# The opening of a fused cross-attention kernel, written in another order

## What is computed

```python
x = x + tanh(g_xattn[0]) * xattn(layernorm(x), ctx, ctx, Wq, bq, Wk, bk, Wv, bv, Wo, bo)
x = x + tanh(g_ffn[0]) * ffn(layernorm(x), Wg, W1, b1, W2, b2)

# xattn
qh = (q @ Wq + bq) per head;  kh = (k @ Wk + bk) per head;  vh = (v @ Wv + bv) per head
attn = softmax(qh @ kh.T / sqrt(16), axis=-1)
return concat(attn @ vh) @ Wo + bo
```

## Time and profile before

| | us |
|---|---|
| median of 3 runs | 1028.3 |
| lowest to highest of them | 1026.89 to 1028.31 |
| profiled execution, its own time | 1025.19 |
| span of the profiled execution | 1023.4 |
| first T product (step -1 opens) | 104.30 |
| first and last output copy of the attention | 120.8, 585.3 |

### The profile page before, as it was taken

One profiled execution on the slowest core, in us unless ns is written; L12 is line 12 of the kernel. 1 busy time (PEld: TensorE's weight loads), 2 busy tenths in 40 slices (PEclk: granted clock), 3 DMA queues, 4 the chain that ended last, 5 costly groups with the idle time before them and its releaser, 6 DMA issues. The chain is left out here.

```text
span 1023.4 us, 23194 instructions
## 1 busy us (share of the span) xinstructions
PE 879.9 (86%) x8875; PEld 697.4 (68%) x8875; DVE 670.4 (66%) x1852; ACT 615.2 (60%) x1312; POOL 242.1 (24%) x208
## 2 busy tenths in 40 slices
PE   4766999999999999999998720169999999999995
PEld 2433676676776676677676510159999999999995
DVE  5424677777777877877878568846647566574440
ACT  1546777777777777777775520056847658476571
POOL 6940000000000000000000031243645556465313
PEclk9989999999999999999999955579999999999998
DMA  5236655655755645745642030132352533525203
GB/s 144 65 75 132 148 124 123 163 122 125 164 119 127 163 114 134 161 114 134 156 106 50 25 101 0 45 121 59 96 130 48 129 100 75 129 47 144 32 11 37
DMA packets 96211, 104.65 MB, mean 102 GB/s; under 512 B 11744, under 2 KB 92272, under 8 KB 96112
## 3 DMA queue, kind: packets, MB, share of 16 engines
q1 hardware_dynamic: 84128, 88.50, 34.6%
q0 software_dynamic: 10752, 14.69, 8.3%
q10 hardware_dynamic: 1232, 0.12, 0.1%
HBM read 39.60 MB, written 14.68 MB: 53 GB/s over the span
## 5 line engine op out<-in xcount | busy, mean ns | idle before, releaser
L361 DVE TENSOR_REDUCE a_nm<-a_pS 112x1 f32<-112x375 f32 x512 | 264.4, 543 | 103.9 <-PE a_pS L537 100.8
L250 ACT ACTIVATE a_P<-a_pT 128x448 f32<-128x448 f32 x384 | 209.1, 546 | 134.5 <-PE a_pT L531 133.6
L537 PE MATMUL a_pS<-a_kst,a_qst 96*112 96x375 bf16 x512 | 151.1, 333 | 3.6 <-DVE a_nm L361 3.0
L531 PE MATMUL a_pT<-a_qst,a_kst 98*128 98x112 bf16 x1536 | 139.0, 213 | 0.1
L531 PEld LDWEIGHTS a_pT<-a_qst,a_kst 98*128 98x128 bf16 x1536 | 107.0, 99 | 40.8 <-issue 8.2
L1250 PE MATMUL e_p<-w2h,e_hh 128*128 128x256 f32 x448 | 128.2, 286 | 0.0
L1250 PE MATMUL e_p<-w2h,e_hl 128*128 128x256 f32 x448 | 126.1, 282 | 0.0
L1250 PE MATMUL e_p<-w2l,e_hh 128*128 128x256 f32 x448 | 126.1, 281 | 0.0
L851 POOL MEMSET r_factors<- 128x1 f32 x15 | 0.6, 102 | 530.1 <-POOLq L62 530.1
L1105 POOL DMA_INDIRECT out_dram<-e_y,e_idx x56 | 88.4, 1578 | 137.5 <-ACT e_y L1134 130.7
L260 ACT ACTIVATE a_kp<-a_pK,a_bk 128x375 bf16<-128x375 f32 x192 | 109.4, 570 | 5.2 <-PE a_pK L564 3.8
(11 more groups left out here) (198 smaller groups left out, 1556.1 us busy)
## 6 DMA issues: line engine op xcount, KB each, us to landing
a_kst<-a_kp SPq DMA_DIRECT2D x192, 192.0 KB, 3.6
w<-in_L_ffn_W_dram SPq DMA_DIRECT2D x16, 1024.0 KB, 7.4
a_qst<-a_qp SPq DMA_DIRECT2D x96, 112.0 KB, 3.8
a_craw<-in_ctx_dram SPq DMA_DIRECT2D x32, 128.0 KB
a_xin<-in_x_dram SPq DMA_DIRECT2D x8, 448.0 KB, 3.9
a_xb<-in_x_dram SPq DMA_DIRECT2D x32, 112.0 KB, 3.0
out_dram<-a_x SPq DMA_DIRECT2D x32, 112.0 KB, 2.4
xn_scratch<-a_x SPq DMA_DIRECT2D x32, 112.0 KB, 2.6
```

Source lines behind the costliest of these rows:

```text
L250: act.activation(P[quad % 2][:, c, :], pT[u % 2][:, 0:4 * LQ], ACT.Exp).then_inc(exp_done, 1)
L361: dve.tensor_reduce(nm[:, h:h + 1], pS[h % 2][0:LQ, 0:LK], AXX, ALU.max, negate=True).then_inc(s_used, 1)
L531: last = pe.matmul(pT[u % 2][:, j * LQ:(j + 1) * LQ], kst[b % 4][:, h, c * 128:(c + 1) * 128], q_of(b, slice(None), h), start=True, stop=True)
L537: pe.matmul(pS[h % 2][0:LQ, 0:LK], q_of(b, slice(0, ROWS), h), kst[b % 4][0:ROWS, h, 0:LK], start=True, stop=True).then_inc(s_ready, 1)
```

## The change

Steps -12 to -2 of the loops are gone (`FIRST = -1`). In front of each engine's loop stands a loop over the query groups j = 0 to 7 of its own. After it, every engine has done for the main loop what it had done before: K of batches 0 to 3, the context transposes of 0 to 4, V of batch 0, all heads of batch 0 and heads 0 to 7 of batch 1 in the first score pass, and the transposed maxima of batch 0. In detail:

- Queries use one bank for each half, pO and pM0 (`pQ = [pO, pM[0]]`), and not two pairs. The third cut of each (`q_low`) is made by VectorE, from the bank.
- K of batches 0 to 3 is computed beside groups 1 to 4, its half t = 1 in bank pS0 and t = 0 in pK. Their semaphores `k_ready` and `k_cut` are one for each half. From batch 4 on all is in pK as before.
- The first score pass of batch 0 is beside groups 5 and 6, the first half of that of batch 1 beside group 7.
- VectorE normalises all of group 0 and the fourth batch of every other group; GpSimd does three batches of groups 1 to 7. GpSimd's fill of the ones rows of kst moves from groups 2 to 5 to groups 4 to 7.
- The xnT copies of groups 6 and 7 are ScalarE's.
- V of batch 0 is made beside group 5, both pieces in pM1. The context transposes of batches 0 to 3 are beside groups 0 to 3.
- SyncE loads two contexts early, and issues all six query stackings of a pair at once for pairs 0 and 1.

The diff, cut to its core:

```diff
-        pQ = [[pS[0], pS[1]], [pO, pM[0]]]
+        pQ = [pO, pM[0]]
...
-        FIRST, LAST = -12, B + 2
-        G, GROUP_0 = B // 4, -10
+        FIRST, LAST, G = -1, B + 2, B // 4
+        EARLY_K, DVE_COPIES = 4, 6
...
+        def k_bank(b, t):
+            return pS[0] if b < EARLY_K and t == 1 else pK
...
+            for j in range(G):
+                if live_q(j + 4):
+                    sp.wait_ge(xnt_ready, 2 * j + 2)
+                    x_group(j + 4)
+                if 2 <= j < 5:
+                    if j == 2:
+                        sp.wait_ge(pads_set, 2)
+                    stack_keys(j - 2)
+                if 1 <= j < 5:
+                    context(j + 1)
+                if j == 1:
+                    stack_queries(0, range(6))
+                if j == 4:
+                    stack_queries(1, range(6))
+            row_max(0)
...
+            for j in range(G):
+                kb = j - 1 if 1 <= j <= EARLY_K else None
+                if 2 <= j <= EARLY_K + 1:
+                    for t in range(2):
+                        k_part(j - 2, t, 2)
+                q_piece(j, 0, 0)
+                if j == 5:
+                    values(0, 0)
+                if kb is not None:
+                    k_part(kb, 0, 0)
+                if live_q(j + 2):
+                    root(j + 2)
+                q_piece(j, 0, 1)
+                q_piece(j, 1, 0)
+                if kb is not None:
+                    k_part(kb, 0, 1)
+                    k_part(kb, 1, 0)
+                if j == 5:
+                    values(0, 1)
+                if DVE_COPIES <= j + 1 < G:
+                    x_copies(act, j + 1)
+                q_piece(j, 1, 1)
+                if j < 4:
+                    ct_copy(j)
+                if kb is not None:
+                    k_part(kb, 1, 1)
...
+            x_statistics(0)
...
+            x_scale(0)
+            for b in range(4):
+                x_norm(0, b)
+            x_statistics(1)
+            x_copies(dve, 0)
+            x_scale(1)
+            for j in range(G):
...
+                if live_q(j + 2):
+                    x_statistics(j + 2)
+                if live_q(j + 1):
+                    x_norm(j + 1, 3)
...
+                maxima(0, 2)
+                if live_q(j + 2):
+                    x_scale(j + 2)
+                maxima(2, 5)
+                if j + 1 < DVE_COPIES:
+                    x_copies(dve, j + 1)
+                maxima(5, 6)
+                q_low(j, 0)
+                maxima(6, 8)
+                if j == 6:
+                    max_parts(0)
+                q_low(j, 1)
...
+                if j == 5:
+                    pe.wait_ge(kst_loaded[0], 96)
+                    pe.wait_ge(qst_loaded[0], 96)
+                    pe.wait_ge(k_cut[1], 3 * EARLY_K)
+                if j == 7:
+                    pe.wait_ge(kst_loaded[1], 96)
+                q_product(j, 0)
+                if kb is not None:
+                    keys(kb, 0, 0)
+                early_s(0, 2)
...
+                q_product(j, 1)
+                early_s(2, 3)
+                q_rest(j, 1, 0)
+                if kb is not None:
+                    keys(kb, 0, 1)
+                    keys(kb, 1, 0)
+                early_s(3, 5)
...
+                if live_q(j + 1):
+                    x_transposes(j + 1)
+                q_rest(j, 1, 1)
+                early_s(5, 6)
+                q_rest(j, 2, 0)
+                if kb is not None:
+                    keys(kb, 0, 2)
+                    keys(kb, 1, 1)
+                if j < 4:
+                    wait(pe, ct_copied, j)
+                    ct_transposes(j)
...
+                early_s(6, 8)
+                q_rest(j, 2, 1)
+                if kb is not None:
+                    keys(kb, 1, 2)
+            pe.wait_ge(ct_copied, 5)
+            m_transpose(0)
+            for t in range(2):
+                pe.wait_ge(q_cut[t], 3 * G)
```

More of the change, by code:

```diff
@@ L209, in _ @@
+                if live(m + 7):
+                    context(m + 7)
                 if live(m + 1):
@@ L552, in weighted, with keys @@
                     last.then_inc(o_ready, 1)
-            def keys(b, i):
-                t, part = divmod(i, 3)
-                wait(pe, k_cut, 6 * b + i)
+            def keys(b, t, part):
+                bank = k_bank(b, t)
+                if part > 0:
+                    pe.wait_ge(k_cut[t], 3 * b + part)
+                else:
+                    wait(pe, k_cut[0], 3 * b + (3 * t if b >= EARLY_K else 0))
+                    wait(pe, k_cut[1], 3 * b)
                 if part == 0:
@@ L609, in _ @@
                     if live(b):
-                        if u == 6 and b == 0:
-                            for t in range(2):
-                                pe.wait_ge(q_cut[t], 3 * (G - 1))
                         if u == 6:
```

303 lines of the change are left out of this document (155 added, 148 removed).

## The result

| | before | after |
|---|---|---|
| median (4 runs each, same chip), us | 1028.3 | 1001.75 |
| lowest to highest | 1026.89 to 1029.24 | 1000.14 to 1002.26 |
| profiled execution, its own time | 1025.19 | 1000.14 |
| span of it | 1023.4 | 998.4 |
| first T product | 104.30 | 76.44 |

The ratio is 0.9741, with a 95% interval of 0.9726 to 0.9755.

A forecast was written before the change was run, and what follows sets the result against it. TensorE bounds the main loop, waits behind ScalarE's K cuts the opening; 2.3 - 3.4 + (52.1 - 24.4) = 26.6 us saved, so 1028.3 - 26.6 = 1001.7, say 1002; range 998 to 1010.

The forecast's parts named there:

- What bounds it, and the sum: TensorE bounds the main loop, waits behind K cuts the opening; 2.3 - 3.4 + (52.1 - 24.4) = 26.6 us gained.
- The start: Start to group 1, VectorE normalising group 0: first query product at 12.3, group 1 at 20.9; gain 2.3 us.
- they will again: In the start: the two query products of group 0 take 5.82 us, as before.
- The K groups: Groups 1 to 4 with K: 6.8 us work plus 1.1 waiting, 7.9 each, 32.4 in all; range 6.8 to 9.5 each.
- Groups 5 to 7: Groups 5 to 7 with maxima, up to the first T product: 24.4 us, before 52.1; bounds 20.2 and 28.
- What is queued behind the new waits: SyncE's query and K stacking between x loads: costed at nothing; uncovered, each would delay its group up to 3 or 4 us.
- The first: Rival: TensorE's clock falls inside the new groups, three to six product pairs, 4.4 to 8.8 us: 1006 to 1011; chance 0.13.
- its step is TensorE's own time, so all of it should come through: Main loop: starts from the same finished pieces at an unchanged step, so the whole 26.6 us gain reaches the total.
- The second: Rival: ScalarE's order keeps K exposed in the groups, two of a batch's six waiting 1.77 us: +10, 1012; chance 0.06.
- The third: Rival: the low clock level holds through the opening, 20.9 to 77.7 us: +36, 1037, slower; chance 0.04.

## Why the prediction was right, step by step

**What bounds it, and the sum.** The main loop kept its pace, so what the opening gained came through, less 1.2 us in step -1, 0.5 over the 31 steps behind it, and 1.2 behind the attention. The first T product moved by 27.9 us where 26.6 was forecast, the span by 25.0. That the median agrees within 0.3 us is partly chance: the profiled execution came out at 1000.14, 1.5 above the forecast 998.6, and the median stands 1.6 above it in place of the assumed 3.1.

**The start.** Forecast: first product at 12.3, group 1 at 20.9, a gain of 2.3. Measured 11.83 and 19.67, a gain of 3.5. VectorE's block took 0.35 us (forecast 0.37), and with group 0 back on GpSimd 2.26 us were lost. Of the 1.2 us beyond, 0.5 lie ahead of the first product; 0.3 of them are there already when the inverse root of group 0 ends (7.80, before 8.14). The larger part, 0.9, comes from "they will again": the two products took 4.94 us (11.83 to 16.77), not 5.82, because the second ran mostly at the full rate. Over the other runs it took 1.81 to 3.11 us, so this is the luck of one execution, about 1 us wide.

**The K groups.** Forecast 7.9 apart and 32.4 in all, by a count of TensorE's issue (6.8) plus one exposed cut (1.1). Measured 7.85 for groups 2 and 3 and 32.0 in all, with 28.30 us busy and one wait of 0.8 a group, in groups 1 to 3 for the cut that was named. The outer two were off in opposite ways. Group 1 took 8.15. Group 4 took 8.14 where the forecast had 8.7, since it copies no context (`if j < 4`), so the wait for that cut falls away in it. With the copy behind that cut the spacing was 7.16, so the reading of ScalarE's list was right. With one bank it was 9.25, near the upper bound of 9.5.

**Groups 5 to 7.** Forecast 8.3, 7.0, 6.5 and 2.6, together 24.4; measured 8.42, 7.17, 6.40 to the transpose at 73.65 and 2.79 from there, together 24.8. With the maxima behind group 7 it was 36.0. The reductions beside the queries are thus worth at most 11.2 of the 26.6 us, and about 9 if what goes with the lower clock in that version is taken off (the estimate above). It is the largest part that was tested alone. VectorE's cut took 0.68 us in place of the forecast 0.62.

**What is queued behind the new waits.** Costed at nothing, and no wait of TensorE for stacked keys, queries or x stands among the waits of 20 to 79 us.

**The rivals.** The first said that the clock would fall inside the new groups, for three to six product pairs. It held 1.00 from 19.67 to 76.44 us. But the mechanism is real and was near: with one bank it fell at group 5, with the maxima behind group 7 it fell at the first score blocks, and in after it fell at a place that no step named, the idle stretch ahead of the first T product. The forecast "its step is TensorE's own time, so all of it should come through" missed this: step -1 took 17.66 us in place of 16.50. The cover was in view: before had step -2's work there, and the edit takes that step away. The loss (1.2) and the better start (1.2) cancel: the prediction was 1.2 us off at each of these two steps, with opposite signs. A rule of the Trainium skill (TensorE: Matmul & The Clock Gate, "A second HAM failure mode: psum-queue depth-cycling") was named for this rival: many short pauses in a kernel that cycles through PSUM banks make the clock swing. After's K groups, 28.30 of 31.99 us busy with a pause in each, kept 1.00, so the trace doesn't agree for this pattern. Another run is nearer to it: with the maxima behind group 7, score blocks in two PSUM banks in turn, with a wait of 0.19 us ahead of nearly every pair, ran at 0.50 from the second pair on, though the clock did not swing there. The falls that the profiled executions of the new opening show from group 1 on followed three things: the idle stretch ahead of the T pass, the row of waits of the version with one bank (0.48, 0.67, 0.82), and in the version with the maxima behind, waits of 0.54, 0.16, 0.20 and 0.94 us within 3 us. Which waits bring the clock down and which don't, these runs leave open.

**The second** rival, K exposed on ScalarE, is out: 4.9 us of waits over eight, 1.1 the longest. **The third**, a low level through the opening, is out too: 1.00 in after from group 1 to the first T product.

**Before's clock.** The prediction gave the clock of before no term of its own; the kernel before with fillers supports that, as far as it goes: 0.9993.

**Left open:** how the 26.6 us divide between the second bank, the interleaving that goes with it, and taking K beside early groups at all, since no run did one without the others from the state before.

## What to carry to other kernels

In a pipeline whose steady state is full, look at the fill: write out both engines' lists for one group of it with durations from the profile. Here the length of a K group came out within 0.1 us for the middle groups and within 0.6 for the outer ones. Where two chains of small items compete, give each half of a chain its own bank and put the other's items between, and move reductions that another engine makes beside products rather than behind them. Then look at the last idle stretch of TensorE ahead of the dense part. Here 2.6 us of idleness cost another 1.2 to 2.6 us behind it at the lower clock. Work or fillers at its beginning avoided that in the four versions that had them; fillers behind its first 1.5 us didn't in the one execution that was traced. And look at the granted clock of every version before its time is put down to its order.

## What the runs showed of the hardware

**VectorE beside GpSimd's memset.** In after, VectorE's normalisation of a 112x256 block took 0.35 us in group 0 and 0.41 at 29.40, with GpSimd idle. Beside one of GpSimd's fills of the ones rows it took 1.03 to 1.45, and ended just behind the fill. VectorE's timeline:

```profile
7.84 1.38 DVE L408 TENSOR_SCALAR a_xin<-a_xin,a_xmv,a_xrs 112x256 f32<-112x256 f32 x4
29.40 0.41 DVE L408 TENSOR_SCALAR a_xin<-a_xin,a_xmv,a_xrs 112x256 f32<-112x256 f32 x1
37.25 1.03 DVE L408 TENSOR_SCALAR a_xin<-a_xin,a_xmv,a_xrs 112x256 f32<-112x256 f32 x1
61.44 1.45 DVE L408 TENSOR_SCALAR a_xin<-a_xin,a_xmv,a_xrs 112x256 f32<-112x256 f32 x1
```

and GpSimd's:

```profile
35.47 2.65 POOL L546 MEMSET a_kst<- 2x3072 int32 x1
60.09 2.65 POOL L546 MEMSET a_kst<- 2x3072 int32 x1
```

The fill at 35.47 ends at 38.12, VectorE's block at 38.28; the fill at 60.09 ends at 62.74, the block at 62.89. The Trainium skill (GPSIMD Engine Reference, "1. Specifications") tells of SBUF interfaces that the two engines share, with contention for some kinds of VectorE's instructions; the trace agrees in kind, though no row tells the kind of this one. It cost nothing on the path: group 6 to the first T product took 16.36 us, and 16.36 also with that block on GpSimd.

**The rate at the start.** The first product of group 0 took 3.33 us in after and the second 1.82, while the same product takes 1.67 from group 1 on. The granted clock reads 1.00 in these stretches all the same, so there the lengths of known products tell the rate, and that row doesn't. In the version with seventy early fillers, where the level had risen and fallen once before these products, the row does show it (0.50 from 14 to 16 us).
